# Degrees by two-level one-hots, two-tensor forms on VectorE and norm statistics in front, in the setup of a graph network kernel

## The reference

```python
# GCN: degrees and their inverse roots
src = jnp.concatenate([edge_index[0], loop])
dst = jnp.concatenate([edge_index[1], loop])
ew = jnp.concatenate([edge_weight, jnp.ones((n,), dtype=edge_weight.dtype)])
deg = jax.ops.segment_sum(ew, dst, num_segments=n)
dis = jnp.where(deg > 0, jax.lax.rsqrt(deg), 0.0)
norm = dis[src] * ew * dis[dst]
...
# attention: one power per edge
att = jnp.power(distance, lam)
...
# SAGE: number of edges of a node
deg = jax.ops.segment_sum(jnp.ones_like(dst, dtype=x.dtype), dst, num_segments=N)
agg = msg_sum / jnp.maximum(deg, 1.0)[:, None]
...
h = jnp.maximum(_layernorm(x, axis=-1), 0.0)          # ahead of each layer
```

## Time and profile before

| | us |
|---|---|
| median of 3 runs | 6867.96 (6860.37 to 6869.52) |
| the profiled execution | 6860.92 |
| its span | 6859.2 |
| first gather of pass 0 starts | 391.95 |
| busy: TensorE / VectorE / ScalarE / GpSimd | 4925.5 / 4014.3 / 1224.3 / 4783.5 |

### The profile page before, as it was taken

One profiled execution on the slowest core, in us unless ns is written; L12 is line 12 of the kernel. 1 busy time (PEld: TensorE's weight loads), 2 busy tenths in 40 slices (PEclk: granted clock), 3 DMA queues, 4 the chain that ended last, 5 costly groups with the idle time before them and its releaser, 6 DMA issues.

```text
span 6859.2 us, 96370 instructions
## 1 busy us (share of the span) xinstructions
PE 4925.5 (72%) x25794; PEld 3252.4 (47%) x25794; DVE 4014.3 (59%) x12497; ACT 1224.3 (18%) x3269; POOL 4783.5 (70%) x4783
## 2 busy tenths in 40 slices
PE   0667777767777676777567777689999984776775
PEld 0444444544444444444344444556666663444444
DVE  7944455544555544555644444578898887444445
ACT  0620000000000100000100000267777763000000
POOL 6157777777777677777677777477777752777774
PEclk9688898888889888888688889899999986889988
DMA  2022222222222222222222222266666641222221
GB/s 56 23 56 53 54 53 53 64 57 53 54 53 53 67 54 53 53 53 53 60 53 53 53 53 53 58 143 146 145 145 145 146 108 28 53 53 53 53 53 48
DMA packets 384024, 466.47 MB, mean 68 GB/s; under 512 B 102957, under 2 KB 289771, under 8 KB 383481
## 3 DMA queue, kind: packets, MB, share of 16 engines
q0 software_dynamic: 152528, 313.83, 18.2%
q1 hardware_dynamic: 201881, 132.45, 7.9%
q10 hardware_dynamic: 29088, 14.03, 0.8%
HBM read 434.51 MB, written 27.81 MB: 67 GB/s over the span
## 4 chain that ended last, share of the span: by engine, by line
POOL 47%; issue 19%; PE 14%; DVE 9%; DMA 8%; ACT 1%; SPq 1%; DVEq 1%; ACTq 0%; POOLq 0%
POOL pool L693 45%; DMA pool<-table,src_col 4%; DMA gath<-table,src_col 3%; POOL gath L672 2%; DVE work L1337 2%; PE psum L834 2%; PE psum L871 2%; PE psum L880 2%; DVE work L1482 2%; PE psum L726 1%; DMA pool<-edge_attr 1%; PE psum L864 1%; PE psum L906 1%; PE psum L808 1%; PE psum L832 1%
## 5 line engine op out<-in xcount | busy, mean ns | idle before, releaser
L693 POOL DMA_INDIRECT pool<-table,src_col x3910 | 3701.0, 947 | 1524.8 <-issue 1146.8
L834 PE MATMUL psum<-pool 128*128 x8300 | 1929.8, 322 | 1394.7 <-DVE pool L1490 1391.6
L834 PEld LDWEIGHTS psum<-pool 128*128 128x128 f32 x8300 | 1700.9, 221 | 2546.8 <-issue 2225.6
L832 PE MATMUL psum<-busy_rows,iota_b 128*128 128x512 bf16 x7820 | 2707.5, 432 | 69.4 <-issue 69.1
L1490 DVE TENSOR_SCALAR pool<-iota_f,rel_col,ew_col 128x128 f32<-128x128 f32 x3320 | 1232.4, 372 | 1800.1 <-SPq L542 1786.7
L672 POOL DMA_INDIRECT gath<-table,src_col x832 | 909.3, 1093 | 257.7 <-issue 224.8
L1482 DVE SCALAR_TENSOR_TENSOR work<-psum,dis,work 128x128 f32 x2490 | 870.7, 350 | 141.7 <-PE psum L834 111.7
L832 PEld LDWEIGHTS psum<-busy_rows,iota_b 128*128 128x128 bf16 x7820 | 850.1, 110 | 179.2 <-issue 92.4
L1490 DVE TENSOR_SCALAR pool<-iota_f,rel_col 128x128 f32<-128x128 f32 x830 | 267.6, 323 | 436.3 <-SPq L542 433.1
L1067 ACT ACTIVATE pool<-psum 128x512 f32<-128x512 f32 (+1 forms) x104 | 58.1, 566 | 1988.8 <-PE psum L796 1988.8
L1067 ACT ACTIVATE pool<-psum,gcn_bias 128x512 f32<-128x512 f32 (+1 forms) x26 | 17.2, 660 | 1937.8 <-PE psum L796 1937.8
(11 more groups left out here) (204 smaller groups left out, 4278.4 us busy)
## 6 DMA issues: line engine op xcount, KB each, us to landing
pool<-table,src_col POOLq DMA_INDIRECT x3910
pool<-edge_attr SPq DMA_DIRECT2D x832, 64.0 KB
pool<-step_masks SPq DMA_DIRECT2D x624, 48.0 KB
pool<-rel_rows SPq DMA_DIRECT2D x208, 128.0 KB
gath<-table,src_col POOLq DMA_INDIRECT x832
table<-work ACTq DMA_DIRECT2D x48, 256.0 KB, 2.3
table<-QV SPq DMA_DIRECT2D x12, 256.0 KB, 2.3
table<-work SPq DMA_DIRECT2D x12, 256.0 KB, 2.3
```

What stands on the lines that cost most here:

```text
L693: gp.indirect_dma_start(out=gath_ring[:, t % RING, :], out_offset=None, in_=source[:, :], in_offset=bass.IndirectOffsetOnAxis(ap=src_col[: ...
L832: pe.matmul(psum[:, SUM_BANKS, :], iota_b[:, :], busy_rows[:, :], start=True, stop=True)
L834: pe.matmul(psum[:, steps.bank(s), 0:D], hot_ring[:, s % HOT_RING, :], gath_ring[:, bass.ds(slots[s % REGS], 1), :].rearrange("p a d -> p ...
```

## The change

- A constant column `consts` (1, 128, 1e30) and `const(k, like)`, which broadcasts it as a tensor. Where the old code has `tensor_scalar` or a copy with the same count, it now has `scalar_tensor_tensor` with such a constant as second tensor (`move` for copies). The conversion of `src` reads and writes with a stride.
- Degrees in two levels: a destination inside its block is 32·low + ... : `low` in 0 to 3 and `high` in 0 to 31. In 8 chunks of 104 steps VectorE makes the one-hots of `high` (104x32, `hot_2`) in one instruction and the parts times the one-hots of `low` (104x4x4, `rhs`) in another. Each step is one product with 32 columns of weights, in the column tile of its quarter. ScalarE makes no one-hots any more; it casts the parts and copies the transposed sums.
- The norm's statistics stand behind the plan, in one run for all 49 blocks; GpSimd's power waits for them (`norm_x.shift`). The plan no longer waits for the weights.
- X is loaded at the head of ScalarE's queue. The six transposes of weights stand ahead of the masks.
- The gathers of `att_rows` stand behind pass 0 on GpSimd, their store behind `count_batches(passes[0])` on SyncE; `att_rows` lies in QV, and VectorE waits for `att_masks_stored` before it writes QV.

```diff
+        def const(k, like):
+            col = consts[0:like.shape[0], k:k + 1]
+            if len(like.shape) == 3:
+                col = col.rearrange("p (a b) -> p a b", a=1)
+            return col.broadcast_to(list(like.shape))
...
         def gpsimd(gp):
...
+            gp.wait_ge(norm_x.shift, NGR)
             gp.tensor_tensor(dist_sb, dist_sb, lam_row, ALU.pow).then_inc(pow_made, 1)
+            gathers(gp, 0, table[0], passes[0])
             gp.wait_ge(att_tiled, 32)
-            gp.wait_ge(offsets_spread, 4)
-            gp.wait_ge(masks_made, 1)
             for i in range(SR):
                 gp.indirect_dma_start(
...
-            for layer in range(3):
+            for layer in range(1, 3):
                 gathers(gp, layer, table[layer % 2], passes[layer])
...
         def tensor(pe):
...
-            for n, (by_vector, by_scalar) in enumerate(DEG_ROUNDS):
...
+            for s in range(NS):
+                i, j = divmod(s, QUADS)
+                k, at = divmod(s, CHUNK)
+                if at == 0:
+                    pe.wait_ge(deg_hot, k + 1)
+                lo = i % PER * PARTS * LOW
+                ins = pe.matmul(psum[HIGH * j:HIGH * (j + 1), i // PER, lo:lo + PARTS * LOW], hot_2[:, k % 2, at, :],
+                                rhs[:, k % 2, at, :, :].rearrange("p k l -> p (k l)"), start=True, stop=True,
+                                tile_position=(0, HIGH * j))
...
+            for k in range(2):
+                pe.wait_ge(deg_t_made, 2 * (k + 1))
+                for n, (j, c) in enumerate((j, c) for j in range(QUADS) for c in range(2)):
+                    for lo in range(LOW):
+                        first = lo * P + HIGH * j
+                        ins = pe.matmul(psum[HIGH * lo:HIGH * (lo + 1), 4 + k, 0:NB], deg_t[0:HALF, k, c, first:first + HIGH],
+                                        block_hot[0:HALF, 2 * j + c, :], start=(n == 0), stop=(n == 7),
+                                        tile_position=(0, HIGH * lo))
+                ins.then_inc(deg_summed, 1)
...
         def vector(v):
...
-            settle()
+            for k, value in enumerate((1.0, float(P), BIG)):
+                v.memset(consts[:, k:k + 1], value).then_inc(consts_made, 1)
+            settle()
+
+            plan_vector(v, own, settle)
             v.wait_ge(weights_loaded, WEIGHTS_LOADED)
             v.tensor_scalar(lam_row, lam_row, lam_col[0:DR, 0:1], None, ALU.add).then_inc(lam_made, 1)
-
-            plan_vector(v, own, settle)
+            v.wait_ge(consts_made, 3)
+            norm_x_vector(v, own, settle)
             step_rows_vector(v, own, settle)
             degrees_vector(v, own, settle)
...
+        def move(v, dest, source):
+            return v.scalar_tensor_tensor(dest, source, 1.0, const(ONE, dest), ALU.mult, ALU.mult)
...
         def step_rows_vector(v, own, settle):
...
+            v.tensor_tensor(rel, tmp, spread(base_of[:, :].rearrange("p (s a) -> p s a", a=1), 2, P), ALU.subtract).then_inc(own.up(), 1)
...
+            v.scalar_tensor_tensor(rel, rel, -1.0, const(TOP, rel), ALU.max, ALU.min).then_inc(own.up(), 1)
...
+            v.tensor_copy(tile_src.rearrange("p s e -> p e s"), tile_src_i.rearrange("p s e -> p e s")).then_inc(own.up(), 1)
...
         def degrees_vector(v, own, settle):
...
+            for k in range(CHUNKS):
+                lo, hi = k * CHUNK, (k + 1) * CHUNK
+                if k >= 2:
+                    v.wait_ge(deg_multiplied, k - 1)
+                v.tensor_tensor(hot_2[:, k % 2, :, :], spread(flat_high[:, lo:hi, :], 2, HIGH),
+                                spread(iota_f[:, 0:HIGH].rearrange("p (a h) -> p a h", a=1), 1, CHUNK),
+                                ALU.is_equal)
+                here = rhs[:, k % 2, :, :, :]
+                v.tensor_tensor(here, spread(parts[:, lo:hi, :].rearrange("p s (k a) -> p s k a", a=1), 3, LOW),
+                                spread(low_hot[:, lo:hi, :].rearrange("p s (a l) -> p s a l", a=1), 2, PARTS),
+                                ALU.mult).then_inc(deg_hot, 1)
```

More of the change, by code:

```diff
@@ L187, in build @@
                 for lo in range(0, SR, GROUP)]
[L190 to L210, removed]
@@ L536, in store @@
                                  source[:, lo:hi, :]).then_inc(stored[which], 16)
[L538 to L544, removed]
+            for nth in range(1, 4):
                 count_batches(passes[nth])
@@ L739, in tensor @@
[L739 to L750, removed]
@@ L955, in scalar @@
+            act.wait_ge(norm_x.var, NGR)
+            act.activation(ln_rstd[:, :], ln_rstd[:, :], ACT.Sqrt).then_inc(norm_x.root, NGR)
+            act.wait_ge(cols_made, len(COLS))
+            for k in range(3):
+                if k > 0:
+                    act.wait_ge(rest_made, k)
+                act.activation(parts[:, :, k].rearrange("p (i j) -> p i j", j=QUADS), by_quarter(ew_col) if k == 0 else rest,
+                               ACT.Copy).then_inc(parts_cast, 1)
             for g in range(NGR):
@@ L1420, in degrees_vector @@
[L1420 to L1426 removed]
+            rel_ij, ew_ij = by_quarter(rel_col), by_quarter(ew_col)
+            v.scalar_tensor_tensor(low, rel_ij, float(HIGH), const(ONE, low), ALU.is_ge, ALU.mult).then_inc(own.up(), 1)
@@ new lines, in degrees_vector, with part @@
+            for k in range(2, LOW):
+                settle()
+                v.scalar_tensor_tensor(low, rel_ij, float(k * HIGH), low, ALU.is_ge, ALU.add).then_inc(own.up(), 1)
+            settle()
+            def part(k):
+                return parts[:, :, k].rearrange("p (i j) -> p i j", j=QUADS)
+            v.wait_ge(parts_cast, 1)
+            v.tensor_tensor(rest, ew_ij, part(0), ALU.subtract).then_inc(rest_made, 1)
+            v.scalar_tensor_tensor(high, low, -float(HIGH), rel_ij, ALU.mult, ALU.add).then_inc(own.up(), 1)
@@ new lines, in degrees_vector @@
+            v.wait_ge(parts_cast, 2)
+            v.wait_ge(rest_made, 1)
+            v.tensor_tensor(rest, rest, part(1), ALU.subtract).then_inc(rest_made, 1)
+            flat_low, flat_high = (t.rearrange("p i (j a) -> p (i j) a", a=1) for t in (low, high))
+            v.tensor_tensor(low_hot, spread(flat_low, 2, LOW), spread(iota_f[:, 0:LOW].rearrange("p (a l) -> p a l", a=1), 1, NS),
+                            ALU.is_equal).then_inc(own.up(), 1)
+            v.tensor_tensor(part(3), const(ONE, low), const(ONE, low), ALU.mult).then_inc(own.up(), 1)
@@ new lines, in degrees_vector @@
+            v.wait_ge(deg_multiplied, CHUNKS)
+            for k_part in range(PARTS):
+                for k in range(DEG_BANKS):
+                    lo, hi = k * PER, min(QS, (k + 1) * PER)
+                    of_part = psum[:, k, 0:(hi - lo) * PARTS * LOW].rearrange(
+                        "p (i k l) -> p i k l", k=PARTS, l=LOW)[:, :, k_part, :]
+                    into = deg_of[:, k_part // 3, lo:hi, :]
+                    if k_part % 3 == 0:
+                        ins = move(v, into, of_part)
+                    else:
+                        ins = v.tensor_tensor(into, into, of_part, ALU.add)
+                if k_part < 2:
+                    ins.then_inc(own.up(), 1)
+                    settle()
```

243 lines of the change are left out of this document (123 added, 120 removed).

## The result

The changed kernel takes 6798.24 us (median of 4 runs, 6794.6 to 6802.07), the one before 6864.16 beside it: a ratio of 0.990, 95% interval 0.9888 to 0.9912. The forecast was 6797. The profiled execution of the changed kernel took 6801.79 us, with a span of 6800.1.

A forecast was written before the change was run, and what follows sets the result against it. GpSimd's gathers were taken to pace the passes, so setup before the first gather counts one for one. Stage times summed to 321.5 us, 70.5 earlier: 6790 against the profiled execution, 6797 against the median; range 6775 to 6850.

The forecast's parts named there:

- T: Start of the plan's first shift (L1275), 21.89 us in the kernel before, forecast at 12.
- P: End of GpSimd's power in the setup, forecast at T + 175.2 = 187.2 us.
- behind the first gather: Rest of the span, from pass 0 on: forecast untouched, so an earlier first gather moves the end one for one.
- Step 1: Setup: the wait for the weights goes behind the plan, so T falls to 12 us, between bounds 8 and 21.9.
- Rival C: Setup: early load buys nothing (T 21.9) and degree products still cost 122 ns; 6865 us, no change; chance 0.04.
- The lock: Setup: GpSimd's power stops VectorE's two-tensor forms, the first subtraction waiting for the power's end; chance 0.78.
- step 2: Setup: norm statistics, 14.6 us, now stand before the power, which starts at T + 47.1 and lasts 128.05 us.
- 2x forms: VectorE's setup instructions that the change turns into two-tensor forms; their loss was to be paid by casts done earlier.
- Rival A: Setup: two-tensor forms run beside the power, so nothing waits for P; 194 us less, 6674; chance 0.15.
- Step 6: Degrees: eight chunks, VectorE 5.25 us each, 832 products at 60 ns, half of the old 122; 55.2 us.
- Step 8: Degrees' second level: 16 transposes, 64 products of 32 columns taken at 8 us; 14.3 us in all.
- Step 5: Front of the degrees: seven steps of 832 at 1.0 us, one of 3328 at 3.5, small ones; 11.3 us.

The follow-up runs named there:

- g3: Changed kernel with X's loads behind the weights in ScalarE's queue and each chunk's degree products 26 in a row in one column tile; 6791.42 us.
- f1: Changed kernel once more, nothing edited; 6811.18 us, ratio 0.9904 to the kernel before.
- f4: Changed kernel with GpSimd's power as two instructions, of 600 and 200 columns; one run, 6776.15 us.
- e4: Changed kernel with the power over only 400 of its 800 columns; one run, 7837.85 us, on a chip where the kernel before takes 8030.1.
- f2: Changed kernel with the power as two instructions of 400 columns; 6723.52 us, ratio 0.9769 to the kernel before.
- g4: Changed kernel, power as 288 and 512 columns not waiting for norm statistics, X's loads behind the weights, small tensors behind pool; 6658.85 us, ratio 0.9689.
- e3: Changed kernel with the strided cast of src (L1403) as a two-tensor move(); 7919.3 us, ratio 0.9862, where the kernel before takes 8030.1.
- f3: Kernel before with only the power split into two instructions of 400 columns; 6755.96 us, ratio 0.9823.
- g1: Kernel before with only 19 unused words per partition placed in front of pool and its neighbours; 6888.29 us, ratio 1.0025.
- g2: Changed kernel with its three small tensors allocated behind pool, restoring the old addresses; 6787.28 us, ratio 0.9877 to the kernel before.

## Why the forecast was right, and where it wasn't

The time came out by luck: some steps were priced too low, others too high, and the sum hid it. By its own steps, from T to the first gather, in the profiled execution (us):

| step | forecast | measured | off |
|---|---|---|---|
| 1, T | 12 | 23.32 | +11.3 |
| 2, power starts at | T + 47.1 | T + 48.2 | +1.1 |
| 2, 3, lock and masks, from P | 14.6 | 3.0 | -11.6 |
| 4, columns | 8.0 | 7.4 | -0.6 |
| 5, front of the degrees | 11.3 | 15.5 | +4.2 |
| 6, chunks | 55.2 | 43.9 | -11.3 |
| 7, reading | 5.9 | 5.8 | -0.1 |
| 8, second level | 14.3 | 6.3 | -8.0 |
| 9, dense step (and small waits) | 25.0 | 23.4 | -1.6 |
| behind the first gather | 6467.3 | 6495.1 | +27.8 |

**Step 1** put the transfer's price too low. "X's load now shares the engines" was named and costed at 4 us; it costs 11.7 (g3). Rival C had this half right: T got no better than 21.9.

**The lock (step 2)** is there, but not as I had taken it: a two-tensor form wasn't held to the end of the instruction. It was held to 82 us at 800 columns (after, f1) and at 600 (f4), not at all at 400 (e4, f2), and for 1.07 us more in one step at 512 (g4), while the power takes 0.16 us a column. The casts of L1337, L1403 and (e3) L1438 are held to the end of an instruction of 800 or 600 columns (before, after, e3, f4). They run freely beside one of 288 or 400 (g4, e4, f2, f3), and beside the 512 of g4 L1438 takes its 0.21 us. Which cast is held isn't told by its speed: unstopped, L1337, one of the prediction's 2x forms, takes 0.61 us and L1403 1.14, and L1378, never stopped, takes 1.08. The 81.8 to 82.2 us are the time of 510 to 514 columns; by the lengths tried, the one from which on VectorE is stopped for long lies above 512 and not above 600. Where between them, and why there, no run shows, nor why a cast is held longer than a two-tensor form. All of it is one operation on float32. The two instructions of the join could hardly have told me: an instruction of 1.38 us that ends 1.24 us behind the product began 0.14 us ahead of its end, and the products last 3.82 and 7.48 us, far less than 82. A lock for the whole instruction, which I had assumed, agrees with the 123.33 us of L1337; the 79.44 us of the subtraction and f3's unstopped cast of 0.61 us don't. Rival A was therefore right about the last third of the power: 11.6 us of masks ran beside it.

**Step 6** was mis-sized because the 122 ns a product that it halves were not TensorE's. In the window of the earlier trace rows VectorE was busy for 101.93 of the 102 us, and its groups there have the one-hots without a gap:

```profile
L1398 DVE TENSOR_SCALAR pool<-iota_b,rel_col 128x128 bf16<-128x128 bf16 x625 | 101.5, 254 | 0.0
```

One each 162 ns, for three products in four, is one product each 122 ns: VectorE's pace. (TensorE counts as busy for 101.14 us there, but the profile models where its products end.) So the stage before gave no price of a product, only a bound, and the row of the load (110) gives none either. The new products, of 32 columns of weights and 16 moving ones, cost 9.6 ns in turning column tiles and 26 in one tile (g3), against the 60 that I took. The stage is VectorE's 5.34 us a chunk, near my lower bound of 5.25. **Step 8** is the same kind of error: its 64 products (128 records) took 1.67 us where I had 8. **Step 5** took steps over 832 strided elements (`by_quarter`) at the 1.0 us of dense ones (L1352: 1.09 for 896); they take 1.56 to 1.60 us.

**Behind the first gather** nothing was costed; by itself this error would have put the time 21 to 28 us above 6797, which the range still covers. I priced what the three new tensors do and not where they lie. Their 19 words move `pool`, into which edge_attr is loaded. From the first gather to the end of the span the profiled executions take: before 6467.3 and (f3) 6472.1; before, shifted, 6497.3 (g1); changed 6495.1, 6492.3 (f1), 6505.2 (f2), 6499.2 (f4) and 6492.1 (g3); changed with the old addresses 6481.6 (g2) and 6485.1 (g4). By these the addresses would account for 25 to 30 us in the kernel before and 7 to 24 in the changed one. But the two executions with before's code and addresses ran 3 and 10 us under the medians of their runs. Taken from the medians, with the first gather of the profiled execution (that of the kernel before at 391.95 on each chip), the stretch is longer than in the kernel before on the same chip by:

| kernel | us |
|---|---|
| 19 words on: after, f1, f2, g1 | 21, 17, 15, 16 |
| as before: f3, g2, g4 | −5, 3, −3 |

So within what the medians can tell, the addresses are the whole of this loss. Why they are slow for the loads wasn't tried; one shift of 19 words was, no other.

The att_rows gathers in the gap cost nothing that shows (pass 0 to pass 1: 991.6 us before, 993.1 after), and products of step 6 never decided, as the bounds said. In the profiled execution +11.3, +5.3 and +27.8 met -33.2: 6801.79 us where the sum gave 6790. That the median hit 6797 within 1.3 us is luck once more: the 7 us added for the kernel before had no counterpart in the changed one, whose profiled execution lay 3.6 us above its median. The chance of 0.78 went to a mechanism of which two thirds were true: 82 of the power's 128 us.

## What to carry to other kernels

If a long GpSimd instruction stands beside VectorE's work, look first at its elements per partition: here two instructions of 400 columns in place of one of 800 gave 1.8% (f3), and the rewriting of VectorE's setup 1.0%. In f2 the second part lost 19.6 us when it was issued into a stretch of two-tensor work without gaps, so place it ahead of one: in g4 it was issued at 97.93, ahead of the chunks at 102.32, and lost about 0.5 us. When a stage is to be the price of a new one, ask first which engine set its pace: the 122 ns a product were VectorE's here. When one new tensor is allocated, compare the stages that the diff doesn't touch, too: the loss lay 4000 us behind the setup that was rewritten. A median that comes out as forecast proves no step; only the stage table does.

## What I had not expected of the hardware

- The lock's length: beside a power of 288, 400 or 512 columns nothing of VectorE was stopped for its length; at 600 and 800 a two-tensor form was held for 82 us, and the casts of L1337 and L1403 to the end of the instruction.
- Its other side, as I read it: a GpSimd instruction of 64.3 us took 83.9 when it was issued into 19.8 us of gapless two-tensor work on VectorE (one case, f2).
- A shift of `gath`, `hot` and `pool` by 19 words in SBUF: 0.25% of the kernel's time (g1), with 32 us more of TensorE's waits for loads of 64 KB into pool (54.3 us against 22.3).
- Products of 32 weight columns and 16 moving ones: 9.6 ns apart in turning column tiles and 26 ns in one, at a granted clock of 0.50.
- A load of X in ScalarE's queue held one small DMA of SyncE's queue for 13.82 us instead of 3.90.
